# Expert rings of two mixture layers: f32 products replaced by three float32r products on weights that are split ahead of time

## The reference

```
x = x + tanh(g_xattn[0]) * L0_xattn(layernorm(x), ctx)
x = x + tanh(g_ffn[0])   * L0_ffn(layernorm(x))
x = x + tanh(g_xattn[1]) * L1_xattn(layernorm(x), ctx)
x = x + tanh(g_ffn[1])   * L1_ffn(layernorm(x))
# L0_ffn: 8 experts, 2 per token, H = 192, no bias, and a shared expert of width 1024
probs = softmax(h @ gate_w.T); topk of 2, renormalised -> cw
act = silu(h @ Wg[e].T) * (h @ Wu[e].T);  out = sum_e cw[:, e] * (act @ Wd[e].T)
# L1_ffn: 16 experts, 6 per token, H = 352, with biases, and a shared expert of width 704
h = silu(xf @ W1.T + B1) * (xf @ W3.T + B3);  y = y + c[:, None] * (h @ W2.T + B2)
```

## Time and profile before

| | us |
|---|---|
| median of 3 runs | 2507.49 (2500.48 to 2511.79) |
| the profiled execution | 2506.47 |
| its span in the trace | 2504.0 |

### The profile page before, as it was taken

The page is one execution under the profiler, slowest core; times in us unless marked ns, Lnnn a source line. Parts: engine busy times, 40 slices in busy tenths (PEclk is TensorE's granted clock), DMA queues, the critical chain, the costliest instruction groups (busy, mean ns, idle before and its releaser), DMA issues.

```text
span 2504.0 us, 37079 instructions
## 1 busy us (share of the span) xinstructions
PE 2107.5 (84%) x9370; PEld 1371.6 (55%) x9370; DVE 1067.8 (43%) x2507; ACT 732.8 (29%) x1105; POOL 747.2 (30%) x534
## 2 busy tenths in 40 slices
PE   5489799788837788888687887999979699999995
PEld 3267678444414555555566664555545356555663
DVE  6754543211128889888467632222212122222221
ACT  4541111122225766565511111222212122122221
POOL 0011000334435767574100102333322233233331
PEclk8699899899976998899889898999989899999998
DMA  3110010555562222220300045343454643434334
GB/s 111 63 66 27 0 51 34 176 93 99 94 149 45 47 36 36 38 40 1 119 27 26 1 172 157 68 83 65 99 164 92 190 90 65 112 66 69 65 69 97
DMA packets 95030, 194.25 MB, mean 78 GB/s; under 512 B 14778, under 2 KB 18746, under 8 KB 94779
## 3 DMA queue, kind: packets, MB, share of 16 engines
q0 software_dynamic: 33600, 79.73, 18.1%
q1 hardware_dynamic: 61242, 112.34, 15.0%
HBM read 943.63 MB, written 61.60 MB: 401 GB/s over the span
## 4 chain that ended last, share of the span: by engine, by line
PE 25%; SPq 17%; issue 5%; DVE 3%; DMA 1%; ACT 1%; POOL 0%; POOLq 0%; DVEq 0%; ACTq 0%
PE ps L1419 9%; PE ps L1441 6%; PE ps L1346 5%; SPq L1166 5%; PE ps L1364 2%; SPq L1162 2%; SPq L1147 2%; SPq L1148 1%; SPq L1149 1%; SPq L1150 1%; SPq L1169 1%; SPq L1151 1%; SPq L1152 1%; SPq L1154 1%; SPq L1156 1%
## 5 line engine op out<-in xcount | busy, mean ns | idle before, releaser
L1419 PE MATMUL ps<-f_wb,f_xT 128*128 x1776 | 564.0, 461 | 2.3 <-ACT f_xT L1267 2.3
L1441 PE MATMUL ps<-f_w2b,f_hT 128*128 x822 | 405.1, 628 | 97.8 <-issue 56.8
L1419 PEld LDWEIGHTS ps<-f_wb,f_xT 128*128 128x128 f32 x1776 | 330.2, 191 | 198.7 <-issue 58.3
L1530 POOL DMA_INDIRECT y_scratch<-f_yo,f_rows x150 | 237.6, 1584 | 441.8 <-ACT f_yo L1273 310.0
L1780 DVE TENSOR_TENSOR f_g<-ps,f_bb 128x352 f32<-128x352 f32 x111 | 58.3, 525 | 586.4 <-PE ps L1419 443.5
L1510 POOL DMA_INDIRECT f_xg<-xn_scratch,f_rows x150 | 159.7, 1064 | 441.1 <-PE ps L1403 220.6
L1441 PEld LDWEIGHTS ps<-f_w2b,f_hT 128*128 128x128 f32 x822 | 151.2, 199 | 244.7 <-issue 244.5
L586 POOL TENSOR_TENSOR a_elo<-a_e,a_ehi 128x768 f16<-128x768 f32 x128 | 218.8, 1719 | 137.5 <-ACT a_ehi L642 135.5
L1273 ACT ACTIVATE f_yo<-ps,f_share 128x512 f32<-128x512 f32 x150 | 103.1, 687 | 356.4 <-PE ps L1441 340.4
L818 DVE TENSOR_REDUCE a_nmax<-ps 128x1 f32<-128x512 f32 x256 | 163.9, 680 | 40.5 <-PE ps L673 40.3
L1346 PE MATMUL ps<-f_xhi,f_w13hi 128*128 128x512 f32 x448 | 175.5, 392 | 2.8 <-POOL f_w13lo L1485 2.8
(11 more groups left out here) (226 smaller groups left out, 3150.7 us busy)
## 6 DMA issues: line engine op xcount, KB each, us to landing
f_wb<-in_f_w_dram SPq DMA_DIRECT2D x216, 2816.0 KB
f_wb<-in_f_w_dram SPq DMA_DIRECT2D x72, 1536.0 KB
f_w2b<-in_f_w_dram SPq DMA_DIRECT2D x261, 256.0 KB
f_bb<-bias_scratch SPq DMA_DIRECT2D x111, 352.0 KB
f_w2b<-in_f_w_dram SPq DMA_DIRECT2D x111, 192.0 KB
f_wraw<-in_f_w_dram SPq DMA_DIRECT2D x14, 768.0 KB, 5.2
xn_scratch<-f_xn SPq DMA_DIRECT2D x32, 256.0 KB, 2.1
y_scratch<-x_res SPq DMA_DIRECT2D x8, 1024.0 KB, 5.3
```

The source lines that it names most:

```text
L1419: mm = pe.matmul(columns((UB if w else GB) + b % 2, H), xT[:, b % 2, k, :], weights(at, w, k), start=(k == 0), stop=(k == KD - 1))
L1441: mm = pe.matmul(ps[:, OB + b % 2, :], hT[:, b % 2, P * j:P * j + P], w2b[:, bass.ds(buf, 1), j, :].rearrange("p o d -> p (o d)"), start=( ...
L1530: pool.indirect_dma_start(y_d, bass.IndirectOffsetOnAxis(ap=rows_of[:, b:b + 1], axis=0), yo[:, b % 3, :], None, bounds_check=ROWS + P - 1 ...
```

## The change

The ring multiplies in float32r. Each f32 product becomes three: high rows by high weights, high rows by low weights, low rows by high weights. The rows are split on the chip: ACT writes the high part (f_xThi, f_hThi) and DVE the difference (f_xTlo, f_hTlo); the f_hT copy that DVE made before is ACT's now.

The weights are split beforehand. A class `Stage` takes the 56 chunks of the weights (12 of layer 0, 44 of layer 1; 768 KB each), rounds them, subtracts, and stores both parts to DRAM scratch, 1 MB of up weights and 512 KB of down weights for a chunk. Its raw and up tiles have two buffers, its down tile has one. 16 chunks are done in `cross_attention_0`, entirely by POOL, with SP's loads and stores; the stage ends when all have landed. 6 are done by POOL at the start of `mixture(0)`, ahead of its own split of the first pair. 34 are spread over the 32 steps of layer 0's shared expert: ACT makes the high parts between its own operations, POOL the low parts behind the low parts of the down weights of each pair.

The ring then fetches whole split experts (2.6 MB in layer 0, 4.5 MB in layer 1) into three buffers, each when the expert three before it is done, without conditions; the tables shrink from nine rows to three. In the ring's block, PE turns the rows of block b+1 ahead of the second up product instead of behind it. SP's writes of the normalised rows, its loads of the next pair's shared weights and its write of the routing weights go to ACT's queue.

```
+        class Stage:
+            def __init__(self, scope, name):
+                self.raw = sb(scope, name + "raw", [P, 2, 1536])
+                self.up = sb(scope, name + "up", [P, 2, 4, 512], F32R)
+                self.down = sb(scope, name + "down", [P, 2, 512], F32R)
...
+            def load(self, sp, i, layer, chunk):
+                if i >= 2:
+                    sp.wait_ge(self.lo_done, i - 1)
+                sp.dma_start(self.raw[:, i % 2, :], a[f"f{layer}_w"][chunk, :, :]).then_inc(self.raw_in[i % 2], 16)
+            def high(self, eng, copy, i):
+                eng.wait_ge(self.raw_in[i % 2], 16 * (i // 2 + 1))
+                if i >= 2:
+                    eng.wait_ge(self.up_out[i % 2], 16 * (i // 2))
+                for w in range(2):
+                    copy(self.part(i, w, 0), self.source(i, w))
+                if i >= 1:
+                    eng.wait_ge(self.down_out, 16 * i)
+                copy(self.down[:, 0, :], self.raw[:, i % 2, 1024:1536]).then_inc(self.hi_done, 1)
+            def low(self, pool, i):
+                pool.wait_ge(self.hi_done, i + 1)
+                for w in range(2):
+                    pool.tensor_tensor(self.part(i, w, 1), self.source(i, w), flt(self.part(i, w, 0)), ALU.subtract)
+                pool.tensor_tensor(self.down[:, 1, :], self.raw[:, i % 2, 1024:1536], flt(self.down[:, 0, :]),
+                                   ALU.subtract).then_inc(self.lo_done, 1)
+            def store(self, sp, i, layer, chunk):
...
+                sp.wait_ge(self.lo_done, i + 1)
+                sp.dma_start(w13_d[layer][e0:e0 + 4, :, blk, :].rearrange("s p n -> p s n"),
+                             flt(self.up[:, i % 2, :, :])).then_inc(self.up_out[i % 2], 16)
...
+                sp.dma_start(w2_d[layer][e0:e0 + 4, r:r + 32, blk // 4, :],
+                             flt(self.down[:].rearrange("p h d -> p (h d)"))).then_inc(self.down_out, 16)
...
 # cross_attention_0, SP
+                for i in range(2):
+                    stage.load(sp, i, *g["PREPARED"][i])
                 sp.wait_ge(zero_set, 1)
+                for e in range(E1):
+                    sp.dma_start(g["w2_d"][1][e, rest:P, HC1 - 1, :], zero[rest:P, :]).then_inc(zero_out, 16)
...
+                sp.wait_ge(zero_out, 16 * (4 + E1))
...
+                for i in range(AT_ONCE):
+                    stage.store(sp, i, *g["PREPARED"][i])
+                    if i + 2 < AT_ONCE:
+                        stage.load(sp, i + 2, *g["PREPARED"][i + 2])
...
+                sp.wait_ge(stage.down_out, 16 * AT_ONCE)
 # cross_attention_0, POOL
+                for i in range(AT_ONCE):
+                    stage.high(pool, pool.tensor_copy, i)
+                    stage.low(pool, i)
...
 # mixture, SP
+                def fetch(e):
+                    sp.dma_start(flt(wb[:, SIZE * (e % 3):SIZE * (e % 3) + 512 * NB]),
+                                 g["w13_d"][layer][e, :, :, :].rearrange("p n j -> p (n j)")).then_inc(w_in, 16)
...
+                for e in range(3, E):
+                    begun = sp.value_load(first_of[0:1, e - 2:e - 1], min_val=1, max_val=BLOCKS)
+                    sp.wait_ge(d_mm, begun)
+                    sp.wait_ge(w_in, 16 * e * LOADS)
+                    fetch(e)
...
 # mixture, ACT, shared expert
+                    more(8 * p)
                     for t in range(1, B):
                         up(p, t)
+                        for s in ((8 * p + 1, 8 * p + 2), (8 * p + 3, 8 * p + 4),
+                                  (8 * p + 5, 8 * p + 6, 8 * p + 7))[t - 1]:
+                            more(s)
...
 # mixture, PE, the ring's products
                     for k in range(KD):
...
+                        for xt, low in ((xThi, 0), (xThi, 1), (xTlo, 0)):
+                            mm = pe.matmul(out, xt[:, b % 2, k, :], weights(at, w, k, low), start=(m == 0),
+                                           stop=(m == 3 * KD - 1))
...
                     for j in range(HC):
...
+                        for ht, low in ((hThi, 0), (hThi, 1), (hTlo, 0)):
+                            mm = pe.matmul(ps[:, OB + b % 2, :], ht[0:n, b % 2, P * j:P * j + P],
+                                           wb[0:n, bass.ds(at + 512 * NB + 1024 * j + 512 * low, D)],
+                                           start=(m == 0), stop=(m == 3 * HC - 1))
...
 # mixture, PE, a block of the ring
+                    pe.wait_ge(xT_lo, b + 1)
+                    pe.wait_ge(w_in, need)
...
+                    if b > 0:
+                        turn_back(b - 1)
+                    if b + 1 < BLOCKS:
+                        turned(b + 1)
                     if BIASED:
-                        if b == 0:
-                            pe.wait_ge(first_w[1], 16)
                         wait(pe, u_read, b - 1)
                         up_blocks(b, 1, at)
-                    if b + 1 < BLOCKS:
-                        turned(b + 1)
```

More of the change, by code:

```diff
@@ L36 @@
 ]
+for m in MOE:
+    m["NB"], m["HC"] = m["H"] // 32, -(-m["H"] // P)
+    m["chunks"] = 2 * m["NB"] * (m["E"] // 8)
+    m["size"] = 512 * m["NB"] + 1024 * m["HC"]
+AT_ONCE = 16
+EARLY = 6
 ROWS = NT * P
@@ L120, in build @@
+        PREPARED = [(0, c) for c in range(MOE[0]["chunks"])] + [(1, c) for c in range(MOE[1]["chunks"])]
         cross_attention_0(nc, a, sb, locals())
@@ L929, in mixture @@
     W13, W2 = 2 * KD * P, D
[L930 to L931 removed]
+    NB, HC, FIRST, SIZE = (cfg[k] for k in ("NB", "HC", "chunks", "size"))
     CHUNKS = FIRST + 2 * PAIRS
[L933 removed]
     REST = H - P * (HC - 1)
[L935 to L936 removed]
+    LOADS = 3
+    LAST_K = P if BIASED else REST
     STEPS = 8 * PAIRS
@@ L1137, in keep @@
                                  x[:, TB * t:TB * t + TB, :]).then_inc(y_out, 16)
+                for s in range(STEPS):
+                    for i in prepared(s):
+                        stage.store(sp, i, *piece(i))
+                        if AT_ONCE + i + 2 < len(g["PREPARED"]):
+                            stage.load(sp, i + 2, *piece(i + 2))
+                    if s == 20:
+                        if BIASED:
+                            sp.wait_ge(brow_out, 16 * 2 * (E // 4))
+                        sp.wait_ge(cw_out, 16)
+                        sp.wait_ge(rows_ready, 1)
+                        sp.wait_ge(table_ready, 1)
+                        fetch(0)
                 keep(0)
@@ new lines, in _ @@
+                sp.wait_ge(w_in, 16 * 2 * LOADS)
+                fetch(2)
+                for e in range(3, E):
[3 more added lines that the diff above has]
+                    fetch(e)
+                if layer == 0:
+                    for i in range(2):
+                        sp.wait_ge(stage.up_out[i], 8 * (len(g["PREPARED"]) - AT_ONCE))
+                    sp.wait_ge(stage.down_out, 16 * (len(g["PREPARED"]) - AT_ONCE))
@@ L1224, in _, with more @@
                     act.activation(red[:], lg[:, :, E], ACT.Exp, scale=-1.0).then_inc(exp_done, 1)
+                def more(s):
+                    for i in prepared(s):
+                        stage.high(act, act.copy, i)
                 def up(p, t):
@@ L1487, in split_lo @@
                                        ALU.subtract).then_inc(w13_ready, 1)
-                for buf in range(2):
-                    pool.memset(w2b[REST:P, buf, HC - 1, :], 0.0).then_inc(w2_clear, 1)
-                    pool.wait_ge(w2_clear, buf + 1)
                 pool.wait_ge(par_in, PARAMS)
                 pool.tensor_copy(tri[:], tri32[:]).then_inc(tri_ready, 1)
+                if layer == 0:
+                    for i in range(EARLY):
+                        stage.high(pool, pool.tensor_copy, i)
+                        stage.low(pool, i)
                 for p in range(PAIRS):
@@ L1507, in _ @@
                         pool.sem_inc(raw_free[h], 1)
+                    for s in range(8 * p, 8 * p + 8):
+                        for i in prepared(s):
+                            stage.low(pool, i)
                 def gather(b):
```

360 lines of the change are left out of this document (165 added, 195 removed).

## The result

| | before | after |
|---|---|---|
| median | 2508.18 us (4 runs, 2500.48 to 2511.79) | 2957.47 us (4 runs, 2952.35 to 2958.76) |
| ratio | | 1.179, 95% interval 1.176 to 1.182 |
| span of the profiled execution | 2504.0 | 2950.5 |

A forecast was written before the change was run, and what follows sets the result against it. PE was taken to bound the rings, and a chain of landed stores the chunk stages. From 2506.47 us, +97 first attention, +31 mixture(0) start, +128 shared expert, -16 and -216 rings gave 2530 us, range 2430 to 2650.

The forecast's parts named there:

- The landing: Stores of each chunk, 1 MB + 512 KB: taken to land in 6.2 us, plus 0.1 for the signals.
- Rival C: Chunks: POOL's roundings and 32-column pieces cost more, landings go by medians; period 13, 105 us more, 2635 us; chance 0.13.
- The chain itself: Chunks: the single down buffer chains rounding, subtractions, store and landing; period 10.9 us with ACT, 11 with POOL.
- The other terms of a chunk: Chunk period besides landing: rounding 0.615 us on ACT or 0.8 on POOL, three subtractions of 1.33 together 4.0.
- Layer 1's ring: Long ring: 111 blocks of 6.67 us plus ends and waits, 765 us against 981.5, so -216.
- 15 for waits on weights: Layer 1's ring: 15 us of waits, as an expert lasts 46 us and its fetch takes some 19.
- Layer 0's ring: Short ring: blocks stay at the scatter chain's 5.67 us; 242 us against 258.8, so -16.
- 9 because the third-next gather waits for SP's last writes of x_res: Layer 0's ring: 9 us added to its 242 for a gather waiting on SP's writes.
- A: Chunks: the 1.5 MB store lands in 5.3 us or less, period 10.0; whole put at 2465 us; chance 0.33.
- turning point: Chunk period of 10.4 us at which the change breaks even, each us of period being 50 us.
- B: Rings' products: a float32r product costs 227 ns whatever its columns up to 512; ring 1 176 us more, 2706; chance 0.12.
- The cover of the second copies: Long ring: products and transposes hide the high and low copies; without it each block pays 1.2 us, 133 in all.

The follow-up runs named there:

- version cut by experts: Changed kernel with each chunk's down store issued as four transfers, one per expert (32 rows of 4 KB), instead of one: 2609.21 us, ratio to before 1.042.
- run with fewer bytes: Kernel with down store split by expert, fetching from the fourth expert on only 5 of 11 (3 of 6) up blocks: 2575.3 us.
- combined version: Changed kernel with per-expert down stores issued first, all splitting on POOL, two down buffers in first attention, chunks 12/3/41, small fetches: 2454.26 us, ratio 0.981.
- last version: Combined version with two chunks of each pair ahead of POOL's down-weight split and zero writes ahead of the stores again: 2409.87 us, ratio 0.963.

## Why the prediction was wrong, step by step

**The landing (the step that failed).** "Landing of 1 MB + 512 KB: ... I take 6.2 and 0.1 for the signals." From the issue of the up store to the next rounding it was 248.03 - 234.70 = 13.3 us. The value came from rows of a write of 1 MB by adding bytes, as if all 16 engines carried each of them. The down store has 4 as its outermost dimension and ran on four engines. In the version cut by experts, where they all carry it, the same term measures 6.3. With 50 periods, 17.7 instead of 10.9 is 340 of the 427 us that the measured time lies above the forecast. The two rings are another 57, and most of the remainder is the rest of the three stages with chunks: a later first store, longer last landings, and the chunks at the start of mixture(0), some of which were 20 to 22 us apart. Rival C had the right place and direction, but took its 13 us from the wrong terms (roundings, pieces of 32 columns, landings by the medians), and its ends didn't reach 17.7.

**The chain itself held.** That the single down buffer makes one chain, that the first attention's end waits for it, that ACT's up steps stand behind stores: shown by the waits and by the version cut by experts, whose period is 10.7 and whose stages are 211.0, 73.3 and 437.0 us where 203, 75 and 431 were forecast. In it only the form and number of the down transfers were changed.

**The other terms of a chunk** were right: rounding on POOL 0.61 (0.8 taken, and at ACT's price), subtractions 1.26 each where nothing disturbs them and 1.28 to 1.38 in the mean, in pieces of 32 columns too (1.33 taken). First store at 36.6 (32 taken).

**Layer 1's ring, 765 forecast, 808.4 measured.** The product (163 against 161) and the block (6.76 against 6.67) were right; this is 10 of the 43. The term "15 for waits on weights" was mis-sized: it took the mean expert of 46 us, but experts differ, and where experts of two blocks (13.5 us) follow each other, the fetch of 17.9 is longer. The run with fewer bytes gave back 28 us.

**Layer 0's ring, -16 forecast, -4 measured.** The failed term is "9 because the third-next gather waits for SP's last writes of x_res". The wait was foreseen, but not that the chunks' stores, ahead of those writes in SP's order, make it longer: 12.64 us of PE's time at this one block. Without the chunks the up products span 231 us instead of 248. No run moves that write alone.

**Rivals.** A (period 10.0) didn't come. Even cut by experts the period is 10.7, above the 10.4 where the forecast put the turning point, and the kernel is slower than before. The combined version wins in another way: ACT is out of the chain, POOL pauses less, and the first attention has two buffers. B (a floor of 227 ns) is refuted by 163. The cover of the second copies held in the long ring: in neither order of the turning does its steady block grow beyond 6.76 us. In the short ring, which the forecast's cover didn't treat, PE waits for f_hTlo 35 times, 20.4 us in all, within blocks that stay at 5.5 to 5.6 us.

## What to carry to other kernels

Estimate a transfer by the engines that can carry it, not by its bytes: look at the outermost dimension of both sides, and at the DMA share in the tail of a landing (0.24 is four engines). A chain through one buffer multiplies every mistake in a landing time by the number of its rounds, so bound that one term by its shape before all others. Work that "has idle engines" still needs the DMA side. An estimate: at the 283 to 304 GB/s of the last version 56 chunks of 2.36 MB take 435 to 467 us, as long as the three stages that should hide them (453 us before), which have transfers of their own.

## What the runs showed of the hardware

A transfer of 4 x 32 rows of 4 KB (512 KB) landed 12.9 us after its issue, at a DMA share of 0.24 in its last 6 us; the same bytes as four transfers of 32 rows landed in 4.1 us each. As two of 2 x 32 rows they made POOL wait for 16.7 us, at a share of 0.13, so both halves lay on the same two engines. A load queued behind the first of these needs 14.0 us instead of 5.8, though most engines are idle. The float32r products of 352 columns start every 163 ns where the granted clock is 1.00 (2.4 GHz), 16 above their columns' 147. The product of 512 had 14 on top, so this is close to a constant and not a floor.
